# A graph network kernel: GpSimd's rests among its indirect gathers are taken out

## What is computed

```python
def conv(h, W, b):
    m = jnp.concatenate([h[dst], h[src], edge_attr], axis=1) @ W + b
    return jax.ops.segment_sum(m, dst, num_segments=n_nodes)
h = jax.nn.relu(conv(x, W1, b1))
h = jax.nn.relu(conv(h, W2, b2))
out = layernorm(x + conv(h, W3, b3))
```

## Time and profile before

| | |
|---|---|
| median of 3 runs | 3054.26 us (3053.72 to 3057.09) |
| profiled execution: time | 3058.39 us |
| its span | 3056.6 us |
| granted PE clock, mean | 0.983 |
| PE busy | 2773.0 us (91%) |
| POOL busy | 2176.2 us (71%) |
| DVE busy | 1580.2 us (52%) |
| DMA traffic | 489.58 MB, mean 160 GB/s |

### The profile page before, as it was taken

How to read it: one execution, slowest core, us unless ns; L and a number is a source line. 1 busy time by engine, 2 the same in 40 slices (tenths; PEclk the granted TensorE clock), 3 DMA queues, 4 the chain that set the end, 5 groups by cost and what they waited for, 6 DMA issues and landing times.

```text
span 3056.6 us, 59532 instructions
## 1 busy us (share of the span) xinstructions
PE 2773.0 (91%) x22952; PEld 1737.1 (57%) x22952; DVE 1580.2 (52%) x3129; ACT 1260.1 (41%) x2314; POOL 2176.2 (71%) x2168
## 2 busy tenths in 40 slices
PE   0049999999999999999968999999998999999998
PEld 0015656565655566565545666666665666666665
DVE  6378999999999999999611111111111111211211
ACT  1049888889898888888500000000000000000000
POOL 2734877787878778787738878777755877877773
PEclk9988999999999999999989999999999999999999
DMA  2143444453535353544586999888888799988882
GB/s 54 34 86 119 127 126 141 115 152 102 162 103 164 103 162 106 158 110 146 164 200 164 214 214 213 218 205 214 213 207 197 182 210 214 209 215 206 215 204 60
DMA packets 248448, 489.58 MB, mean 160 GB/s; under 512 B 161870, under 2 KB 197545, under 8 KB 220045
## 3 DMA queue, kind: packets, MB, share of 16 engines
q1 hardware_dynamic: 141766, 272.31, 33.7%
q10 hardware_dynamic: 58404, 143.10, 17.2%
q0 software_dynamic: 48000, 70.35, 11.9%
HBM read 341.83 MB, written 143.70 MB: 159 GB/s over the span
## 4 chain that ended last, share of the span: by engine, by line
PE 63%; DVE 22%; POOL 8%; issue 4%; ACT 2%; DMA 1%; SPq 0%; ACTq 0%; POOLq 0%; DVEq 0%
PE ps L1099 29%; PE ps L1107 16%; DVE is_key L916 9%; PE ps L1080 6%; DVE is_low L906 4%; POOL far_rows L677 4%; PE ps L1131 3%; PE ps L1160 3%; DVE masks L924 2%; POOL blocks L663 2%; ACT blocks L753 2%; PE ps L1161 2%; DVE far_masks L939 2%; PE ps L1121 2%; PE ps L1135 1%
## 5 line engine op out<-in xcount | busy, mean ns | idle before, releaser
L677 POOL DMA_INDIRECT far_rows<-parts,far_src x1350 | 1481.0, 1097 | 517.2 <-issue 378.0
L1099 PE MATMUL ps<-blocks,parts 125*128 125x375 fp8e4 x7500 | 1544.7, 324 | 3.8 <-ACT blocks L753 2.1
L753 ACT ACTIVATE blocks<-ps 125x505 fp8e4<-125x505 f32 x1875 | 1111.5, 787 | 141.8 <-PE ps L1080 141.8
L1099 PEld LDWEIGHTS ps<-blocks,parts 125*128 125x128 bf16 x7500 | 740.5, 100 | 421.7 <-issue 19.8
L1080 PE MATMUL ps<-is_key,is_low 128*125 128x505 bf16 x1875 | 720.5, 393 | 29.6 <-DVE is_key L916 14.2
L916 DVE TENSOR_SCALAR is_key<-from_one,parts 128x500 bf16<-128x500 f16 x1875 | 696.0, 419 | 25.7 <-PE ps L1080 19.7
L1107 PE MATMUL ps<-blocks,parts 125*64 125x375 fp8e4 x7500 | 685.8, 326 | 0.0
L1107 PEld LDWEIGHTS ps<-blocks,parts 125*64 125x64 bf16 x7500 | 398.5, 110 | 275.0 <-issue 154.1
L976 DVE COPY z<-ps 125x256 f32<-125x256 f32 x75 | 31.5, 420 | 899.1 <-PE ps L1161 862.4
L1080 PEld LDWEIGHTS ps<-is_key,is_low 128*125 128x125 bf16 x1875 | 257.7, 138 | 258.6 <-DVE is_key L916 100.9
L939 DVE SCALAR_TENSOR_TENSOR far_masks<-far_dst,from_one 128x2250 fp8e4<-128x2250 int32 x75 | 187.7, 2502 | 325.3 <-PE ps L1135 321.0
(11 more groups left out here) (102 smaller groups left out, 1521.0 us busy)
## 6 DMA issues: line engine op xcount, KB each, us to landing
blocks<-counts SPq DMA_DIRECT2D x100, 1066.4 KB
counts<-blocks ACTq DMA_DIRECT2D x25, 4101.6 KB
blocks<-counts SPq DMA_DIRECT2D x100, 984.4 KB
far_rows<-parts,far_src POOLq DMA_INDIRECT x1350
blocks<-counts SPq DMA_DIRECT2D x100, 123.8 KB
counts<-blocks ACTq DMA_DIRECT2D x25, 476.1 KB
blocks<-counts SPq DMA_DIRECT2D x100, 114.3 KB
attr_stage<-in_edge_attr SPq DMA_DIRECT2D x125, 88.0 KB
```

Of the source, the lines that this page charges most:

```text
L677: nc.gpsimd.indirect_dma_start(far_rows[:, g % 2, j, :], None, parts_d[layer], bass.IndirectOffsetOnAxis(ap=far_src[:, g % BATCHES, j:j + ...
L753: nc.scalar.activation(blocks[0:L, b % 2, :, n * W:(n + 1) * W], build[0:L, c % BUILD, 0:COLS].rearrange("p (t w) -> p t w", w=W), ACT.Cop ...
L1099: nc.tensor.matmul(acc_ps(g), parts[0:L, layer % 2, t, 0:2, :].rearrange("p k d -> p (k d)"), blocks[0:L, g % 2, t, :], start=(t == 0), st ...
```

## The change

The list of pauses becomes empty, so `gather_batch` calls `rest()` nowhere:

```diff
@@ -45,7 +45,7 @@
     COLUMNS = (TILES + 1) * DENSE
     BLOCK = -(-COLUMNS // 4) * 4
     WORDS = TILES * DENSE // 2
-    PAUSES = [0, 6, 12]
+    PAUSES = []
     QUARTERS = [0, 24, 50, 74, TILES]
     J = 11
     FJ = 18
```

## The result

The changed kernel takes 3051.40 us (median of 19 runs), the kernel before 3057.63 in as many: the ratio is 0.998, 95% interval [0.9973, 0.9987]. The change saves 6.2 us (4 to 8 by the interval), where I had said 10.7. The profiled execution of the changed kernel has a time of 3051.40 and a span of 3049.5 us.

The account below looks back on a forecast made before the run. PE sets the pace in long stretches, POOL in the first three batches of layers 1 and 2. Gains of 6.7 us in layer 1 and 4.0 in layer 2 sum to 10.7: 3058.39 - 10.7 = 3047.7, or 3043.6 from 3054.26; range 3039 to 3052.

Parts of the forecast that it names:

- the sum of all low ends: Low ends of the gains at the six far-sum waits together: 6.4 us, or 3047.9.
- the rival of the engines: DMA engines, not POOL's issue, set every landing; only batch 25 gains, 2 to 3 us, 3051.8; chance 0.14.
- the bounds of my own sum: All high to all low ends of the gains at the six waits: 3040.2 to 3047.9; forecast with these bounds, chance 0.74.
- batch 25: Start of layer 1: issue counts, two rests give POOL a lead, and the far sum's wait falls by 1.86 us.
- The long stretches are worth nothing.: Layers 1 and 2 beyond each start: PE is busy throughout, so removed rests only lengthen POOL's wait; saving nothing.
- What a rest costs POOL, 0.93 us: On POOL in layers 1 and 2: each rest costs 0.93 us, a batch with three of them 2.8 us.
- Batch 26, 1.6 us: Far sum in layer 1: gain between 1.2 us if engines limit and 2.78 if POOL does; taken as 1.6.
- Batch 27, 2.13 and 1.09 us: Layer 1: the whole 2.13 us wait goes, and the 24 slower matmuls behind it save 1.09 us.
- Batch 50, 1.2 us: Start of layer 2: two rests count, at most 1.86 of a 1.92 us wait, low end 0.5; taken as 1.2.
- Batches 51 and 52, 1.2 and 1.6 us: Layer 2: batch 51 gains 1.2 us (bounds 1.0 and 2.78); batch 52's wait of 1.61 goes, low end 0.8.
- Its first rest stands ahead of the wait ..., and is hidden before and after: Batch 25 on POOL: the rest before the wait for stored features is hidden, so only two rests count, 1.86 us.
- The full queue: Rival: back-to-back gathers fill their queue and stall POOL, up to 171 us slower, 3225; chance 0.08 including another unfound loss.

Follow-up runs that it names:

- the first two experiments: Against the kernel before: no rests in the first three batches of layers 1 and 2, ratio 0.9977; rests only in those batches, ratio 0.9995.
- The cut block loads: SP loads 16 of 125 partitions of each block quarter in layers 1 and 2: 3016.53 us without rests (0.9867 to before), 3027.74 with rests (0.9903).
- the other two without rests: The changed kernel repeated, 3049.61 us, and the kernel before without rests in the first three batches of layers 1 and 2, 3051.21 us.
- the store first: Changed kernel with SP waiting for layer 0's stored features before loading batch 26's blocks: 3035.66 us; with the three rests, 3043.57 us.

## Why the prediction was wrong

The direction was right, and so was where the gain lies. The size was not: 6.2 us and not 10.7, below even the sum of all low ends, 6.4. That the time of 3051.40 lies within 3039 to 3052 is due to the room given to the rival of the engines; the bounds of my own sum ended at 3047.9. Those bounds started from 3054.26, the median of the kernel before in 3 runs, which is 3057.63 in 19.

The step that failed is how much an earlier issue is worth where block loads lie in the way, at batches 26 and 50. In distances, the terms measured 1.8 at batch 25, -0.1 at 26, 3.0 at 27 with what stands behind it, -0.7 at 50, and 2.5 at 51 and 52 together, 6.5 in all. Of the 4.2 us that this is short of 10.7, 3.6 are missing at 26 and 50. By its own steps, the means of the table standing for what was measured:

- **The long stretches are worth nothing.** Right, shown by the first two experiments: 132 rests there, 0.9995.
- **What a rest costs POOL, 0.93 us.** Right. From the first gather of batch 25 to sum 25 it is 25.78 with two rests and 24.00 without, 1.78 against 1.86 forecast.
- **Batch 26, 1.6 us, "1.2 us is what remains when the engines are the limit".** This is the step that failed. Sum 26 comes 27.9 us after sum 25 with rests and 28.0 without: nothing. I took the 83 packets left at 1626 us and let them move at q0's best rate, 58 a us. The rate wasn't the trouble. What I left out is that the burst of block loads goes with PE's arrival and not with POOL: issued earlier, the gathers don't find the same free engines earlier. In the changed kernel 192 packets were left at 1622, behind that burst, and then moved at 50 a us beside ACT's stores. The cut block loads show it: there PE goes on 2.1 us after the last gather is issued, here 5.1 to 5.3.
- **Batch 27, 2.13 and 1.09 us.** The distances 26 to 27 and 27 to 28 fell by 1.5 and 1.55, 3.0 against 3.2. The wait at 27 went as forecast. The slow matmuls went too, but others came: PE's granted clock after a wait of 18.7 us (stretches of the changed kernel, columns as above):

```profile
1598.00:1601.00 3.00, 3.00 (x37) 2.63 (x37) 0.00 (x0) 0.00 (x0) 2.39 (x3) 0.50 0.24 52
1604.00:1608.00 4.00, 4.00 (x38) 2.33 (x36) 0.00 (x0) 0.00 (x0) 3.09 (x4) 1.00 0.19 40
```

0.50 is the lower of the two levels, 1.2 GHz, and from 1604 on it is the upper one, 2.4. The slow phase lasted longer after these waits than before (the 24 matmuls behind sum 25 took 5.04 us against 4.09 before, those behind sum 26 4.77 against 4.05). It cost 1.7 us in the changed kernel's profile and 1.5 and 1.0 in the other two without rests, while 1.09 was saved behind batch 27 and another 0.47 in the far sum itself. I had counted only the saving. Why it lasted longer is open: the waits themselves had become shorter.
- **Batch 50, 1.2 us.** Failed in the same way: no gain. Sum 50 comes 44.3 us after sum 49 with rests (43.97, 44.57) and 45.0 without (45.73, 44.20, 45.03); the two groups overlap, so a loss isn't shown. Its last gather was issued at 2335.11 in the changed kernel and at 2343.89 before, 3.0 us earlier counted from sum 49, and PE went on 7.1 us after it instead of 2.3. That block loads are the cause here is inferred from batch 26 and from sum 51 with the loads cut; at sum 50 itself PE didn't wait there.
- **Batches 51 and 52, 1.2 and 1.6 us.** 50 to 51 fell by 1.9 and 51 to 52 by 0.6: 2.5 against 2.8.
- **"Its first rest stands ahead of the wait ..., and is hidden before and after".** Said of batch 25, where the plain kernels neither bear it out nor refute it (39.0 to 40.3 us in both groups). At batch 50, where I also counted two rests only, it is wrong: the gather behind such a rest starts later by 0.9 us (17.2 against 16.35 on the mean). That helped the change and was not in my sum.
- **Layers.** Layer 1: 4.7 of the 6.7 forecast. Layer 2: 1.8 of 4.0.

Of the rivals, "the engines, not POOL, set every landing" was the one that came nearest at batches 26 and 50, and was wrong at 25, 27 and 51. The full queue did not show: POOL's gathers without rests start 1.25 us apart, as forecast, but for at most one of 2 to 3.2 us in a batch, as before. The rule of the Trainium skill, "DMA: Bandwidth & Descriptors", section "Queues, rings and completion order", that a DMA engine takes turns packet by packet between queues, would have let q0 move beside q1. The changed kernel's 32 packets against 114 in 4 us don't bear it out at this place either. But it isn't refuted: with the store first, while block loads ran on for long, q0 moved 219 packets beside 237 of q1. POOL issues some 24 packets a us, about what moved, so this fits the rule without proving it. What rows 8 caught is the start of a burst: there q0 stood nearly still for some 3 us with work outstanding. I took one such window for the whole behaviour.

## What to carry to other kernels

A transfer issued earlier lands earlier only if the engines have room at that moment. Before counting the lead as a gain, shift the whole timetable of the other queues, which here follow the engine that waits, and see what lies between the new issue and the old landing. A saving on an engine that is not the bound is worth something only where that engine starts late, so look first at why it starts late: here one wait in SP's queue was worth 15 us, twice what all the rests cost, and far sums done later 34 us. And a distance between two events, in several profiles of each kind, showed a microsecond that the times of single runs, 12 us apart at the extremes, could not.

## What the runs showed of the hardware

- **Gathers nearly stand still at the start of a burst of large loads, and get a packet for a packet later.** In 4 us q0 moved 17 packets beside 106 of q1, and 32 beside 114 in the changed kernel. There, from 1618.9 to 1620.9 us, it moved 2 beside 68, with 64 to 126 packets issued and not yet moved. With block loads running on for long it was 219 beside 237 (store first). In 2 us with 16 packets of q1 it moved 116.
- **A small store takes long beside large loads of another queue.** Issued at 1549.99 on ACT's queue, it let POOL start only at 1575.16, while q1 took 93% of the engines; 746 packets of the store's queue moved beside 787 of q1. With q1 held back POOL started at 1556.50.
- **A rest that ended 40 us ago still delays the waiting gather behind it at the start of layer 2**, by 0.9 us on the mean of 3 profiles against 5 (and 0.5 between the two with cut block loads, 15.20 and 14.73). At the start of layer 1 it doesn't show. The mechanism is open.
- **A queue can refuse to take a transfer for long**: two pairs of issues took 18.0 and 15.9 us on ACT where 0.84 is usual. Seen in one kernel, cause open.
